# Cross-attention in steps of 512 queries instead of 256, with one probability buffer refilled in place

## The reference, cut to what matters

```
qh = _split_heads(jnp.einsum('bnq,qi->bni', x, Wq))          # x: 4 x 512 x 256
kh = _split_heads(jnp.einsum('bmc,ci->bmi', context, Wk))    # context: 4 x 1024 x 192
vh = _split_heads(jnp.einsum('bmc,ci->bmi', context, Wv))
sim = jnp.einsum('hid,hjd->hij', qh, kh) * SCALE             # 8 x 2048 x 4096
mean = jnp.mean(sim, axis=-1, keepdims=True)
sim = (sim - mean) * ATTN_MATRIX_SCALE + mean
attn = jax.nn.softmax(sim, axis=-1)
out = jnp.einsum('hij,hjd->hid', attn, vh)
...
return jnp.einsum('bni,iq->bnq', out, Wout) + bout
```

## Time and profile before

| | |
|---|---|
| time, median of 3 runs | 2642.66 us (2639.93 to 2644.95) |
| time of the profiled execution | 2639.82 us |
| its span, first to last instruction | 2637.7 us |
| mean granted TensorE clock | 0.991 of 2.4 GHz |
| busy: PE / PEld / DVE / ACT / POOL | 97% / 87% / 73% / 61% / 5% |
| HBM traffic over the span | 57 GB/s |

### The profile page before, as it was taken

How to read it: one execution, slowest core, us unless ns; L and a number is a source line. 1 busy time by engine, 2 the same in 40 slices (tenths; PEclk the granted TensorE clock), 3 DMA queues, 4 the chain that set the end, 5 groups by cost and what they waited for, 6 DMA issues and landing times. The chain is left out here.

```text
span 2637.7 us, 47104 instructions
## 1 busy us (share of the span) xinstructions
PE 2551.6 (97%) x17680; PEld 2291.6 (87%) x17680; DVE 1926.4 (73%) x3632; ACT 1608.6 (61%) x3051; POOL 138.3 (5%) x161
## 2 busy tenths in 40 slices
PE   7799979999999999999999999999999999999998
PEld 5699968998899889998999889988998899889987
DVE  6588867776777777776777677767776777677787
ACT  5699845566566646565556566556665556656566
POOL 2353010000000000000000000000000000000003
PEclk9899989999999999999999999999999999999999
DMA  7896442001200120003000200012001200110000
GB/s 220 222 191 143 94 157 80 17 16 65 73 17 16 47 82 17 21 12 119 18 17 17 107 31 17 16 57 73 17 24 57 73 17 16 64 67 17 28 1 33
DMA packets 93854, 156.54 MB, mean 59 GB/s; under 512 B 42576, under 2 KB 56080, under 8 KB 93680
## 3 DMA queue, kind: packets, MB, share of 16 engines
q1 hardware_dynamic: 89680, 141.20, 17.9%
q0 software_dynamic: 3248, 12.72, 1.6%
q10 hardware_dynamic: 752, 0.26, 0.0%
HBM read 122.56 MB, written 27.39 MB: 57 GB/s over the span
## 5 line engine op out<-in xcount | busy, mean ns | idle before, releaser
L1623 ACT CAST pt_hi<-xt_ps 128x512 fp32r<-128x512 f32 x1024 | 592.9, 585 | 568.2 <-PE xt_ps L1593 552.3
L1702 DVE TENSOR_TENSOR pt_lo<-xt_ps,pt_hi 128x512 fp32r<-128x512 f32 x1024 | 704.7, 688 | 255.2 <-ACT pt_hi L1623 251.7
L1691 DVE TENSOR_SCALAR_CACHE_REDUCE xprobs<-xs_ps 128x1024 f32<-128x1024 f32 x512 | 626.7, 1224 | 176.0 <-PE xs_ps L1533 171.5
L1604 PE MATMUL xo_ps<-pt_hi,v_hi 128*128 128x256 f32 x2048 | 647.4, 316 | 2.4 <-DVE pt_lo L1702 2.3
L1629 ACT ACTIVATE xprobs<-xprobs,xneg_max 128x1024 f32<-128x1024 f32 x512 | 591.4, 1155 | 27.3 <-DVE xneg_max L1697 27.3
L1593 PE MATMUL xt_ps<-ident,xprobs 128*128 128x128 f32 x4096 | 603.8, 272 | 0.0
L1604 PE MATMUL xo_ps<-pt_hi,v_lo 128*128 128x256 f32 x2048 | 571.3, 279 | 0.0
L1604 PE MATMUL xo_ps<-pt_lo,v_hi 128*128 128x256 f32 x2048 | 570.0, 278 | 0.0
L1593 PEld LDWEIGHTS xt_ps<-ident,xprobs 128*128 128x128 f32 x4096 | 484.1, 140 | 61.9 <-issue 6.7
L1604 PEld LDWEIGHTS xo_ps<-pt_hi,v_hi 128*128 128x128 f32 x2048 | 386.3, 189 | 5.8 <-DVE pt_lo L1702 2.6
L1604 PEld LDWEIGHTS xo_ps<-pt_lo,v_hi 128*128 128x128 f32 x2048 | 388.3, 190 | 2.0
(11 more groups left out here) (236 smaller groups left out, 2699.7 us busy)
## 6 DMA issues: line engine op xcount, KB each, us to landing
v_split<-ctx_split SPq DMA_DIRECT2D x68, 768.0 KB, 5.8
xq<-x_split SPq DMA_DIRECT2D x64, 512.0 KB, 3.3
q_st<-rel_split SPq DMA_DIRECT2D x32, 256.0 KB, 4.2
q_st<-q_split SPq DMA_DIRECT2D x32, 192.0 KB, 4.6
k_st<-k_split SPq DMA_DIRECT2D x32, 192.0 KB, 5.0
ctx_split<-ctx_out POOLq DMA_DIRECT2D x8, 768.0 KB, 4.1
q_split<-stage_hi SPq DMA_DIRECT2D x8, 512.0 KB, 4.7
k_split<-stage_hi SPq DMA_DIRECT2D x8, 512.0 KB, 4.8
```

The source lines that it names most:

```text
L1604: last = pe.matmul(o_ps[:, 0:GQ], v[:, vs], pt[:, c % 3, GQ * j:GQ * (j + 1)], start=c == 0 and j == 0 and m == 0, stop=c == PIECES - 1 an ...
L1623: act.copy(pt_hi[:, c % 3, :], t_ps[:, c % 3, :]).then_inc(t_rounded, 1)
L1691: dve.tensor_scalar(probs[:, par if kind == "A" else 1 - par, t, CHUNK * i:CHUNK * (i + 1)], s_ps[:, buf, :], LOGIT, None, ALU.mult, ALU.m ...
L1702: dve.tensor_tensor(pt_lo[:, c % 3, :], t_ps[:, c % 3, :], pt_hi[:, c % 3, :].bitcast(F32), ALU.subtract).then_inc(t_ready, 1)
```

## The change

A step now takes 512 queries (four tiles, t = 0 to 3), so a head has 4 steps and the whole 32. `xprobs` is one buffer, `[P, QI, KEYS]` with QI = 4, of the same size as before, and holds one step. It is refilled in place: the keys are taken in quarters of 1024, in the order 2, 3, 0, 1 (`QUARTERS`); when a quarter has been transposed for all four tiles (a phase, 8 pieces), the next step's scores of that quarter are written over it in the phase behind. Scores of the quarter that is transposed last, key quarter 1, are computed behind all `T` of the step (`last_scores`); only then is a row's maximum known, and the exponentials can start. Those of the first phase's quarter stand between the steps, in halves of 512 columns; those of the other three quarters are taken during the step, one phase ahead of their `T`.

A piece is now one key tile by 512 queries: four transposes as before, and three matmuls of 512 columns. `W c` stands three pieces behind `T c` (`LAG`). `O` and `out` handle 512 queries at a time, queries are projected for the next step in the first phase, in two halves. A next head's `K` and `V` are spread over the head's last step, the last two `V` behind its last `W`. All loops are written out. In the channel mix's first part, tiles 12 to 15 have all their moments taken after the cross-attention (before, 14 and 15), `own` and four `norm` move from ACT to DVE, and there are three groups of square roots instead of two.

```
-            probs = keep.enter_context(nc.sbuf_tensor("xprobs", [P, 2, 2, KEYS], F32))
+            probs = keep.enter_context(nc.sbuf_tensor("xprobs", [P, QI, KEYS], F32))
...
+QUARTERS = (2, 3, 0, 1)
+LAG = 3
+def quarter_items(s, phase, extra):
+    items = []
+    for c in range(EACH * phase, EACH * (phase + 1)):
+        items.append(("T", s, c))
+        if c >= LAG:
+            items.append(("W", s, c - LAG))
+        items += extra.get(c - EACH * phase, [])
+    return items
+def exponents(s, phase):
+    return {c: [("E", s, t, phase)] for t, c in enumerate((1, 2, 4, 5) if phase == 1 else (0, 2, 4, 6))}
+def chunk_scores(s, phase, at=(1, 3, 5, 7)):
+    return {c: [("A", s, t, QUARTERS[phase])] for t, c in enumerate(at)}
+def last_scores(s, weights):
+    items = []
+    for t in range(QI):
+        items.append(("A", s, t, QUARTERS[3]))
+        if t >= 1:
+            items += [("M", s, t - 1), ("E", s, t - 1, 0, 0), ("E", s, t - 1, 0, 1)]
+    items += weights[:1] + [("M", s, QI - 1), ("E", s, QI - 1, 0, 0), ("E", s, QI - 1, 0, 1)] + weights[1:]
+    return items
+def step_items(s):
...
+    if s >= 1:
+        more[0] = {0: [("O", s - 1)], 3: [("out", s - 1)]}
+    if not final:
+        more[0] = both(more[0], {1: [("Q", s + 1, 0)], 6: [("Q", s + 1, 1)]})
+        more[1] = chunk_scores(s + 1, 0)
+        more[2] = chunk_scores(s + 1, 1)
+        more[3] = chunk_scores(s + 1, 2)
+    if head_end and not final:
+        more[0] = both(more[0], {2: [("K", h + 1, 0)], 5: [("K", h + 1, 1)]})
...
+    items += last_scores(s + 1, weights)
+    if head_end:
+        items += [("V", h + 1, 2), ("V", h + 1, 3)]
...
+            def turn(s, c):
+                at = s * PIECES + c
+                if c % EACH == 0:
+                    pe.wait_ge(exped, EXPED[s, c // EACH, 0])
+                if c == EACH // 2:
+                    pe.wait_ge(exped, EXPED[s, 0, 1])
+                if at >= 3:
+                    pe.wait_ge(t_ready, at - 2)
...
+            def weigh(s, c):
+                if c == 0 and s >= 1:
+                    pe.wait_ge(o_ready, s)
...
+                pe.wait_ge(t_ready, at + 1)
+                for m, (v, pt) in enumerate(((v_hi, pt_hi), (v_hi, pt_lo), (v_lo, pt_hi))):
+                    last = pe.matmul(o_ps[:], v[:, P * kt:P * (kt + 1)], pt[:, at % 3, :], start=c == 0 and m == 0,
+                                     stop=c == PIECES - 1 and m == 2)
```

More of the change, by code:

```diff
@@ L1237, in rest_of_mixed, with both @@
                           ALU.subtract).then_inc(done, 1)
[L1240 to L1260, removed]
+NORM_TILES = (range(0, 2 * QI), range(2 * QI, 3 * QI), range(3 * QI, NT))
+LAST_TILES = NORM_TILES[2]
+STEPS = T // N
+PIECES = KEYS // P
+QUARTERS = (2, 3, 0, 1)
+EACH = PIECES // len(QUARTERS)
+LAG = 3
+ALL_STEPS = XH * STEPS
+IS_CHUNK = ("A", "out", "Q", "K", "V", "MT")
+def quarter_items(s, phase, extra):
[6 more added lines that the diff above has]
+    return items
+def both(*parts):
     out = {}
@@ L1275 @@
[L1275 to L1300, removed]
@@ new lines, with numbered, exps_of @@
+ITEMS = before_items()
+for _s in range(ALL_STEPS):
+    ITEMS += step_items(_s)
+def numbered(kinds):
+    return {item: n for n, item in enumerate(item for item in ITEMS if item[0] in kinds)}
+CHUNK_AT, KV_AT, EXP_AT = numbered(IS_CHUNK), numbered(("K", "V")), numbered(("E",))
+V_AT = numbered(("V",))
+def exps_of(s, phase, half=1):
+    return max(n for item, n in EXP_AT.items() if item[1] == s and (item[3], item[4:]) <= (phase, (half,) if phase == 0 else ())) + 1
+EXPED = {(s, phase, half): exps_of(s, phase, half) for s in range(ALL_STEPS) for phase in range(4) for half in range(2 if phase == 0 else 1)}
@@ new lines, in _ @@
+            make = {"A": scores, "Q": project_q, "K": project_k, "V": project_v, "out": project_out, "MT": turn_first}
+            for item in ITEMS:
+                kind = item[0]
+                if kind in IS_CHUNK:
+                    if CHUNK_AT[item] >= 2:
+                        pe.wait_ge(freed, CHUNK_AT[item] - 1)
+                    make[kind](item).then_inc(filled, 1)
+                elif kind == "T":
+                    turn(*item[1:])
+                elif kind == "W":
+                    weigh(*item[1:])
@@ L1799, in channel_mix @@
         act_hi, act_lo = sb("act_hi", [P, 2, CH, N], F32R), sb("act_lo", [P, 2, CH, N], F32R)
-        relu, square, gate, gated = (mix.late[:, 2 * n:2 * n + 2, :] for n in range(4))
+        relu, square, gate, gated = (mix.late[:, n] for n in range(4))
         w_hi, w_lo = mix.w_hi, mix.w_lo
```

646 lines of the change are left out of this document (294 added, 352 removed).

## The result

The kernel after takes 2695.3 us (median of 4 runs, 2685.5 to 2699.0) against 2641.8 for the kernel before: a ratio of 1.019 (95% interval 1.0175 to 1.0206), slower by 1.9%. The prediction was 2688, range 2655 to 2725. The profiled execution took 2696.3 us, 56.5 more than the one of before.

The account below looks back on a forecast made before the run. The prediction took PE's matmul columns as the bound. Stalls of 86.0 us after against 40.9 before add 45 us to the profiled 2639.8, giving 2685, or 2688 for the runs; range 2655 to 2725.

Parts of the forecast that it names:

- What bounds the kernel: Cross-attention before the change: within a head PE does not wait; a step costs its columns, 30.8 us.
- Wider matmuls worth nothing: `W` matmuls: three of 512 columns take 0.70 us, six of 256 take 0.71, so no gain.
- The step end: PE between steps: 1.8 us waiting for exponentials, 0.5 behind that, 0.1 for banks; 2.4 us where it cost nothing.
- ramp: PE from `T 0` to `W 0` of a new step: waits of 0.25 for piece 0's slot and 0.25 for `O`.
- The phases cost nothing: Inside a step's phases: no other stalls, since DVE's 9.5 us of load hides under PE's 14.7.
- slack: Pieces inside phases: `pt_lo` is ready before its slot is wanted, by 0.7 us without score chunks, over 2 with them.
- The sum: Whole kernel: stalls of 86.0 us after against 40.9 before, 45 us added, 2688 us for the runs.
- A: Rival on step ends: they are covered and old stalls go, so the kernel is faster, 2628 us; chance 10%.
- break-even: Step ends: the change wins once an end costs under 1.0 us.
- D: Rival on step ends: no difference, an end at 1.0 us, 2643 us; chance 4%.
- C: Rival on step ends: they cost 1.5 to 3 us more each, 2735 to 2785 us, taken as 2750; chance 12%.
- B: Rival on `W`: the wide matmul is cheaper, 0.48 us a piece, 490 us in all, near 2250; chance 3%.

Follow-up runs that it names:

- e9_o_first: Kernel after with an early maximum over half the keys, no scores between steps, queries-first opening, `O` ahead of an exponential, two score chunks between: 2633.2 us.
- e2_w_256: Kernel after with each 512-column `W` matmul split into two of 256 columns, all else kept: 2700.9 us.
- e8_exact_best: Kernel after with maxima and halves right behind each tile's last score chunk, queries-first opening, tile 3's second half behind the first cast: 2660.3 us.
- e1_max_first: Kernel after with each tile's maximum and two half-exponentials right behind that tile's own last score chunk: 2648.9 us, 1.0036 of before.
- e10_all_keys_max: Kernel after with maxima and halves right behind each tile's last score chunk, and the queries-first opening; all 4096 keys in the maximum: 2648.3 us.
- e3_max_last: Kernel after with all four maxima and all eight half-exponentials moved behind the last score chunk: 2831.3 us, 1.0718 of before.
- e4_max_of_half: Kernel after with the maximum over 2048 keys only, first-phase maxima and half-exponentials moved into the last phase of the step before: 2813.4 us.

## Why the prediction was right, point by point

*What bounds the kernel.* PE's columns, and nothing else before: right. `e9_o_first` keeps all work in the new tiling and comes back to 61.75 us a step.

*Wider matmuls worth nothing:* right, 9.4 us by the trace of `e2_w_256`, 0.35% of the time. The busy figures, which would have promised 490, are the trap that the distances avoid. The Trainium skill's sustained gap of 131 ns for 512 columns (page TensorE: Matmul & The Clock Gate, section Back-to-back issue gap) is borne out by none of these traces, which show 0.23 us; the isolated gap of the same section, 216 ns by its formula, is the nearer one.

*The step end.* Predicted 2.4 us as 1.8 + 0.5 + 0.1. Measured: 63.95 - 61.6 = 2.35, of it 1.74 gap and 0.5 ramp. The halves block ACT for 0.70 as taken from the earlier trace rows. The chain through maximum and seven halves is shown by moving it both ways. The ramp's 0.5 is right in size and in part by luck. I made it up of two waits of 0.25, `T 3` for the slot of piece 0 and `W 0` for `O`. PE's rows show no wait of `T 3`, and its weight loads about 0.15 to 0.2 for `O`; the rest is that I took eight transposes in a row for twice four, 0.70, where they take 0.79 even in the kernel before. Nor does the ramp hang on tile 3's second half, as I had it: the first cast waits for the first piece's own transposes (`e8_exact_best`).

*The phases cost nothing:* right for the kernel as it stands, but the slack that I named was smaller than it sounds: 0.7 us more on ACT in the first phase costs 0.5.

*The sum.* The table compares the terms with the differences between the two profiled executions, stretch by stretch.

| stretch | predicted | measured |
|---|---|---|
| up to the first `K`, same instructions | 0 | +2.9 |
| first `K` to first `T`, less five more score chunks (7.0) | +1.6 | +5.2 |
| first `T` to last `W`, with those 7.0 added back | +40.9 | +44.1 |
| behind the last `W` | +2.6 | +4.3 |
| all | +45 | +56.5 |

Between the first `T` and the last `W` a head is 5.2 us longer (279.7 against 274.5) where I had 4.9, 2.1 in seven heads; the other 1.1 lie in the last head. In the opening I counted no wait for the second half of the queries, and this execution has one of 4.2 us. It is not shown to be an effect of the change: `e2_w_256`, with the same order there, has none, and its opening is 1.5 us longer than before by the same reckoning, near the 1.6 predicted. Behind the last `W`, 2.4 of the 4.3 us are the clock: windows of the kernel after and of `e1_max_first`, a few us behind the last `W`:

```profile
2645.00:2650.00 5.00, 4.45 (x17) 3.83 (x18) 4.38 (x13) 2.95 (x6) 0.00 (x0) 0.66 0.02 7
```

```profile
2600.00:2610.00 10.00, 8.93 (x58) 8.02 (x59) 9.53 (x18) 8.75 (x17) 3.24 (x2) 1.00 0.01 3
```

With 1.00 there that run takes 52.2 us from the last `W` to the end where the kernel after takes 54.6 and the kernel before 50.3. So the edit costs 1.9 (2.6 predicted), and the clock came on top: it is 54.5 us or more from the last `W` to the end in each profiled execution in which the granted clock fell twice there (five besides the kernel after), 53.9 where it fell once (`e10_all_keys_max`), and 52.2 or 52.3 in the four where it did not. The +2.9 up to the first `K` is no effect of the change: over the runs, whose instructions there are the same, that point lies between 377 and 385 us. So of the 11 us by which the profiled execution passes the sum, about 9 differ from execution to execution with the instructions unchanged.

*The rivals.* A (ends covered) did not happen: an end costs 2.35 us, over the break-even of 1.0. But the wait was set by where `M` stands, and I had followed that order without asking what another would give: with one reordering (`e1_max_first`) an end costs 1.05, which is D's case, 2643 by the sum and 2648.9 measured. C did not happen; `e3_max_last` shows what it would have looked like, with a clock drop that I had not priced. B falls by `e2_w_256`, and D for the kernel as it stands.

## What to carry to other kernels

Where a buffer is refilled in place, look for the one result that needs the last piece of the old round (here a row maximum): its chain stands bare once a round, and the order of the small instructions in it decides between 0.5 and 4.6 us. In lists that several engines walk in step, look for rings over two queues: in `e4_max_of_half` DVE's maximum stood behind a piece's subtraction, and ACT's exponentials, which wait for that maximum, stood ahead of the cast that DVE's next subtraction waits for. Such a ring costs its whole length each turn, with each engine idle while the other works. Price matmuls by distances between starts.
